# Layer 1 of a two-layer graph attention: two rows of 2048 values made on 128x16 tiles and carried by transfers

## What is computed

```
Wh  = h @ W                              # (B, 2048, 256)
s_i = Wh @ a[:256]                       # a node's own term
s_j = Wh @ a[256:]                       # its term as a neighbour
e   = leaky_relu(s_i[:, :, None] + s_j[:, None, :], 0.2)
e   = where((adj > 0) | eye, e, -inf)
h'  = elu(softmax(e, -1) @ Wh)
out = layernorm(h + h')
```

## Time and profile before

| | |
|---|---|
| median of 3 runs | 4035.5 us (4033.26 to 4039.04) |
| the profiled execution | 4037.52 us |
| its span, first to last instruction | 4035.0 us |
| mean granted TensorE clock | 0.975 |
| layer 0 | to about 2698 us |
| start of layer 1: mask and first batch's preparation | 2698 to 2813 us |
| layer 1's eight batches | 2813 to 4035 us |
| one batch | about 156 us |
| busy over the whole span | PE 3749.1, DVE 3096.8, ACT 2503.3, POOL 2038.1 us |

### The profile page before, as it was taken

How to read it: one execution, slowest core, us unless ns; L and a number is a source line. 1 busy time by engine, 2 the same in 40 slices (tenths; PEclk the granted TensorE clock), 3 DMA queues, 4 the chain that set the end, 5 groups by cost and what they waited for, 6 DMA issues and landing times. The chain is left out here.

```text
span 4035.0 us, 71120 instructions
## 1 busy us (share of the span) xinstructions
PE 3749.1 (93%) x25476; PEld 1764.5 (44%) x25476; DVE 3096.8 (77%) x4053; ACT 2503.3 (62%) x3554; POOL 2038.1 (51%) x1068
## 2 busy tenths in 40 slices
PE   6999999999999999999999999952998998899998
PEld 1333323333323332332333333321776777777777
DVE  6676777677577677677767757858889889899897
ACT  3565656566666566566656566631676776776777
POOL 1776777677677677677767768842011011011010
PEclk9999999999999999999999999976999999999999
DMA  5000000001000000000000100023110110111101
GB/s 213 1 32 12 22 33 12 12 14 41 12 12 32 22 12 33 12 22 33 12 12 13 42 12 12 22 96 139 32 53 26 49 53 22 53 40 35 32 24 39
DMA packets 106437, 141.08 MB, mean 35 GB/s; under 512 B 3793, under 2 KB 87633, under 8 KB 104017
## 3 DMA queue, kind: packets, MB, share of 16 engines
q1 hardware_dynamic: 104816, 135.80, 10.1%
q10 hardware_dynamic: 1248, 0.40, 0.1%
HBM read 102.63 MB, written 33.55 MB: 34 GB/s over the span
## 5 line engine op out<-in xcount | busy, mean ns | idle before, releaser
L368 ACT ACTIVATE probs<-probs 128x1024 f32<-128x1024 f32 x1024 | 1080.4, 1055 | 945.9 <-DVE probs L621 915.4
L621 DVE SCALAR_TENSOR_TENSOR probs<-sc_ps,clip_hi 128x1024 f32<-128x1024 f32 x1024 | 1203.2, 1216 | 572.8 <-PE sc_ps L446 568.9
L267 POOL TENSOR_TENSOR psums<-probs 128x1024 f32<-128x1024 f32 x512 | 1246.6, 2457 | 163.4 <-ACT probs L368 163.4
L1075 PE MATMUL out_ps<-wh,e 128*128 128x257 f32 x4096 | 964.6, 389 | 166.0 <-DVE e L1217 159.9
L446 PE MATMUL sc_ps<-q_cols,k_cols 64*128 64x512 f32 x4096 | 1022.3, 617 | 25.1 <-DVE probs L621 12.6
L462 PE MATMUL ctx_ps<-probs,v_rows 128*32 128x512 f32 x8192 | 977.3, 595 | 1.2 <-DVE seg_ctx L544 1.2
L1075 PEld LDWEIGHTS out_ps<-wh,e 128*128 128x128 f32 x4096 | 778.1, 193 | 326.8 <-DVE e L1217 120.6
L278 POOL TENSOR_TENSOR ctx_t<-ctx_t,seg_ctx 128x1024 f32<-128x1024 f32 x224 | 534.2, 2385 | 604.5 <-DVE seg_ctx L544 604.4
L446 PEld LDWEIGHTS sc_ps<-q_cols,k_cols 64*128 64x128 f32 x4096 | 353.1, 186 | 698.0 <-issue 575.4
L904 POOL TENSOR_TENSOR rstd<-var_eps,minus_half 128x4 f32<-128x4 f32 x32 | 68.4, 2138 | 1069.9 <-DVE var_eps L1177 1069.9
L462 PEld LDWEIGHTS ctx_ps<-probs,v_rows 128*32 128x32 f32 x8192 | 255.8, 110 | 597.8 <-issue 550.2
(11 more groups left out here) (85 smaller groups left out, 2393.8 us busy)
## 6 DMA issues: line engine op xcount, KB each, us to landing
x_cols<-in_xT SPq DMA_DIRECT2D x8, 2048.0 KB, 10.2
probs<-in_adjT SPq DMA_DIRECT2D x16, 1024.0 KB, 8.4
x_rows<-in_x SPq DMA_DIRECT2D x32, 512.0 KB, 4.8
x<-res SPq DMA_DIRECT2D x32, 512.0 KB, 3.3
x_in<-x SPq DMA_DIRECT2D x8, 2048.0 KB, 10.9
x_res<-x SPq DMA_DIRECT2D x32, 512.0 KB, 4.6
out<-h SPq DMA_DIRECT2D x32, 512.0 KB, 3.2
e<-in_adjT SPq DMA_DIRECT2D x8, 1024.0 KB, 7.9
```

The costliest lines, as they stand in the source:

```text
L267: pool.tensor_tensor(psums[:, q % 2, pair, :], probs[:, (SJ * q) % RING, pair, :], probs[:, (SJ * q + 1) % RING, pair, :], ALU.add).then_i ...
L368: act.activation(probs[:, n % RING, pair, :], probs[:, n % RING, pair, :], ACT.Exp, scale=DH ** -0.5).then_inc(s_exp, 1)
L621: dve.scalar_tensor_tensor(out=probs[:, n % RING, pair, :], in0=sc_ps[:, p, :, :], scalar=-LIM, in1=clip_hi[:, j, c * CW:(c + 1) * CW][:, ...
L1075: last = pe.matmul(out_ps[:, bank(c, t), 0:F + 1], e[:, n % ERING, t * P:(t + 1) * P], wh[:, p, j, 1:F + 2], start=(j == 0), stop=(j == JB ...
```

## The change

The own terms s_i are no longer made by products of their own. W a1 becomes one more column of w_ext, so that each of the 16 products for wh has 258 columns and gives s_i beside s_j, with i along the partitions (wh[:, p, j, 0]). The four uses of PE, ACT's four copies and s_row are gone. SyncE carries s_i to memory, as 2048 single values, and back as a 128x16 tile with node 16 q + r in partition q (`spread_own`, in chunk 2). After the reduction it carries the maxima out of partition 0 of low into the same form, m_c (`make_rows`, in the last chunk). VectorE does the four row operations on 128x16, all behind step 54. SyncE then stores the two rows in memory and loads each back into all 128 partitions, and ACT waits for these loads.

```diff
-    TU, WU, SU = KB * NC, JB, NC
-    USES = TU + WU + SU
+    TU, WU = KB * NC, JB
+    USES = TU + WU
+    RJ = N // P
...
-    ROWS_AT = (53, 55, 57, 59)
+    ROWS_AT = 54
...
+            def spread_own(b):
+
+                sp.wait_ge(s_prepread, count(b, USES, 2 + TU + WU))
+                with nc.allow_non_contiguous_dma(reason="2048 values a batch"):
+                    sp.dma_start(s_d[0].rearrange("(j p) -> p j", p=P), wh[:, b[1] % 2, :, 0]).then_inc(s_sout, 16)
+                sp.wait_ge(s_sout, count(b, 16, 16))
+                sp.dma_start(s_c[:, :], s_d[0].rearrange("(p j) -> p j", p=P)).then_inc(s_sin, 16)
+
+            def make_rows(b):
+                p = b[1] % 2
+                sp.wait_ge(s_all, count(b, 1, 1))
+                sp.dma_start(m_c[:, :], low[0:1, p, :].rearrange("o (q j) -> o q j", j=RJ)).then_inc(s_m, 16)
+                sp.wait_ge(s_rows, count(b, 4, 4))
+                sp.dma_start(rows_d.rearrange("r (p j) -> p r j", p=P), rows_c[:, :, :]).then_inc(s_rout, 16)
+                sp.wait_ge(s_rout, count(b, 16, 16))
+                sp.dma_start(best[:, p, :], rows_d[0].partition_broadcast(P)).then_inc(s_rin, 16)
+                sp.dma_start(low[:, p, :], rows_d[1].partition_broadcast(P)).then_inc(s_rin, 16)
...
+                    if c == 2 and more:
+                        spread_own(following(b))
+                    if c == NC - 1 and more:
+                        make_rows(following(b))
...
-                    act.wait_ge(s_rows, count(b, 4, 4))
+                    act.wait_ge(s_rin, count(b, 32, 32))
...
-                else:
-                    c = u - TU - WU
-                    for k in range(KB):
-                        last = pe.matmul(prep_ps[:, u % 2, :], wa1_b[:, k, :],
-                                         x_cols[:, k, c * CW:(c + 1) * CW],
-                                         start=(k == 0), stop=(k == KB - 1))
...
                 if k == 0:
-                    dve.wait_ge(s_prepread, count(b, USES, 2 + USES))
-                    dve.wait_ge(s_all, count(b, 1, 1))
-
-                    dve.tensor_tensor(low[:, p, :], low[:, p, :], s_row[:, :], ALU.add).then_inc(s_rows, 1)
+                    dve.wait_ge(s_sin, count(b, 16, 16))
+                    dve.wait_ge(s_m, count(b, 16, 16))
+                    dve.tensor_tensor(m_c[:, :], m_c[:, :], s_c[:, :], ALU.add).then_inc(s_rows, 1)
...
-                            if n in ROWS_AT:
-                                row_operation(following(b), ROWS_AT.index(n))
+                            if n == ROWS_AT:
+                                for k in range(4):
+                                    row_operation(following(b), k)
```

More of the change, by code:

```diff
@@ L681, in _, with layer1 @@
             run(dve, prologue, chunk, tail)
-def layer1(nc, x1, adjT, W, a, out):
+def layer1(nc, x1, adjT, W, a, s_d, rows_d, out):
     B, N, F = x1.shape
@@ L759, in layer1 @@
         x_cols = sb("x1_cols", [P, KB, N])
-        wh = sb("wh", [P, 2, JB, F + 2])
+        wh = sb("wh", [P, 2, JB, F + 3])
         s_fifth = sb("s_fifth", [P, 2, JB])
-        s_row = sb("s_row", [P, N])
+        s_c = sb("s_c", [P, RJ])
+        m_c = sb("m_c", [P, RJ])
+        rows_c = sb("rows_c", [P, 2, RJ])
         best = sb("best", [P, 2, N])
@@ L863, in prologue @@
                 load_x((0, 1))
+                spread_own((0, 0))
+                make_rows((0, 0))
             def steps(b, chunks, prev, more):
@@ L1024, in _ @@
             pe.wait_ge(s_id, 4)
-            pe.wait_ge(s_wa, 2 * KB + KB)
+            pe.wait_ge(s_wa, 2 * KB)
             def prepare(b, u):
@@ L1092, in _ @@
             for k in range(KB):
-                for i, (row, dst) in enumerate(((a1_r, wa1[:, k:k + 1]), (a2_r, w_ext[:, k, 0:1]))):
-                    dve.tensor_tensor_reduce(out=trash[:, 2 * k + i, :], in0=w_ext[:, k, 1:F + 1], in1=row[:, :],
+                for i, (row, dst) in enumerate(((a1_r, w_ext[:, k, 0:1]), (a2_r, w_ext[:, k, 1:2]))):
+                    dve.tensor_tensor_reduce(out=trash[:, 2 * k + i, :], in0=w_ext[:, k, 2:F + 2], in1=row[:, :],
                                              scale=1.0, scalar=0.0, op0=ALU.mult, op1=ALU.add,
                                              accum_out=dst).then_inc(s_wa, 1)
[L1097 to L1101, removed]
             def mask_piece(i):
@@ L1123, in maximum @@
                 if j == 0:
-                    dve.tensor_scalar(best[:, p, :], mask[:, 0, :], wh[:, p, 0, 0:1], None, ALU.min)\
+                    dve.tensor_scalar(best[:, p, :], mask[:, 0, :], wh[:, p, 0, 1:2], None, ALU.min)\
                        .then_inc(s_best, 1)
@@ L1143, in row_operation @@
                     dve.wait_ge(s_rows, count(b, 4, 2))
-                    dve.tensor_tensor(best[:, p, :], s_row[:, :], low[:, p, :], ALU.subtract).then_inc(s_rows, 1)
+                    dve.tensor_tensor(rows_c[:, 0, :], s_c[:, :], m_c[:, :], ALU.subtract).then_inc(s_rows, 1)
                 if k == 3:
-                    dve.scalar_tensor_tensor(out=low[:, p, :], in0=s_row[:, :], scalar=ALPHA, in1=low[:, p, :],
+                    dve.scalar_tensor_tensor(out=rows_c[:, 1, :], in0=s_c[:, :], scalar=ALPHA, in1=m_c[:, :],
                                              op0=ALU.mult, op1=ALU.subtract).then_inc(s_rows, 1)
@@ L1256, in build @@
     layer0(nc, x, xT, adjT, wqT, wkT, wvT, woT, bq, bk, bv, bo, gamma, beta, x1)
-    layer1(nc, x1, adjT, W, a, out)
+    s_d = nc.dram_tensor("s_own", (1, x.shape[1]), F32, kind="Internal").ap()
+    rows_d = nc.dram_tensor("rows", (2, x.shape[1]), F32, kind="Internal").ap()
+    layer1(nc, x1, adjT, W, a, s_d, rows_d, out)
 def kernel(x, adj, L0_gnn_Wq, L0_gnn_bq, L0_gnn_Wk, L0_gnn_bk, L0_gnn_Wv, L0_gnn_bv, L0_gnn_Wo, L0_gnn_bo,
```

39 lines of the change are left out of this document (18 added, 21 removed).

## The result

| | before | after |
|---|---|---|
| median | 4035.9 us (4033.3 to 4039.0, 4 runs) | 3989.3 us (3986.9 to 3994.0, 4 runs) |
| profiled execution, span | 4037.5, 4035.0 us | 3986.9, 3985.0 us |
| mean granted TensorE clock | 0.975 | 0.972 |

The ratio is 0.9886, with a 95% interval of 0.9868 to 0.9903: 46.7 us by the medians, 50.0 us between the two profiled executions. 3996 us was forecast, with 3979 to 4024 as the range.

A forecast was written before the change was run, and what follows sets the result against it. Row operations, ACT, VectorE's masks and TensorE in turn were taken to bound each batch boundary. Boundaries -48.3, clock +5, start +4.0 and nothing exposed at L = 10.5 gave -39.3 us: 3996 us, range 3979 to 4024.

The forecast's parts named there:

- The chain at the boundary: Last chunk: row operations, then ACT, VectorE's masks, TensorE set the time; shortening the row operations gains 6.9 us a boundary.
- The two bounds that I found close together: At a boundary: ACT after nmr lets PE go on at 3279.9; TensorE's own unbroken work needs until 3280.24.
- L: Time from the last row operation to the rows' landing in all partitions: 10.5 us, of which store 2.2, load 8.3.
- the factor of 1.35 for the shared source: In the load: all partitions reading one place lengthens the bytes' time, from packets of 64 ns against 48.
- The hidden part: At each boundary L may be 10.9 us at no cost; each us above costs a us at seven boundaries.
- The rival of the slow shared reads: Rival (3): the two loads from one place run under 190 GB/s; at 134, L 19.7, +31.5, 4067 us; chance 0.11.
- the prediction's formula: Whole change: -48.3 + 5 + 7 x max(0, L - 10.9) + (L - 6.5); zero at L = 15.8.
- The products at no gain: Third chunk: TensorE's 16 removed instructions a batch gain nothing, as PE catches up during VectorE's 4.09 us mask at step 49.
- The clock: TensorE's new idle pieces before steps 44 and 49 bring low-clock stretches at three boundaries more: +5 us (0 to +12).
- The start: Start of layer 1, before the first batch: nothing hides the chain of transfers, L - 6.5 = +4.0 us.
- SyncE's queue: Two added waits, all hidden: own terms' store takes 3 to 16 us, with 21.9 us free before chunk 1's store.

The follow-up runs named there:

- the run with short row operations: The kernel before, its four row operations on 16 of 2048 columns, no transfer added: 3977.9 us, ratio to before 0.9856.
- the small store twice: The changed kernel with the store of the two rows done a second time after the first has landed: 3996.3 us, ratio 0.9907.
- Loads made twice: The changed kernel with the two loads into all partitions done again after the first pair has landed: 4038.2 us, ratio 1.0006.
- the products kept: The changed kernel with TensorE's four uses for the own terms and ACT's four copies put back, result unused: 3989.2 us, ratio to before 0.9882.

## Why the prediction was right

**The chain at the boundary** (row operations, ACT, masks, TensorE) was the right reading. 6.9 us a boundary were forecast. The last chunks gave 7.1 and the first chunks behind them another 0.13. The two bounds that I found close together, nmr at 19.77 us behind the reciprocals and TensorE unbroken, are both in the trace: 19.37 us, and PE at work from 3238.65 to 3269.17. That the chain without transfers gives this gain, the run with short row operations shows.

**L** was forecast at 10.5 us and measured 8.6 to 9.5 (16.7 to 17.6 us less 8.07; this counts to ACT's start, some 0.2 us behind the landing). The store took 1.6 and not 2.2 us, the load 7.0 to 8.0 and not 8.3. The mistake in this term was the factor of 1.35 for the shared source. It came from rows of 1 KB, and at 8 KB there is none. The 64 and 48 ns were means over 104 and 173 packets, with those of 4 bytes among them: of both kinds most packets of 1 KB lasted 46 ns, and a few long ones made the difference. The hidden part was forecast at 10.9 and is 10.2. The landing was hidden by 0.7 to 1.6 us, so at the boundaries these errors did not reach the sum. In part that is luck: at the L of 10.5 that I took, 0.3 us a boundary would have shown. And the chain was one store of 1.6 us from showing, as the small store twice has it.

**The rival of the slow shared reads** (3) did not come about at 8 KB. Its mechanism is real, though, and shows at 2 KB. At the 108 GB/s that the 2 KB loads had, 2 MB would take 19.4 us (an estimate), and by the prediction's formula the change would have lost. Loads made twice took the gain to nothing at a mean L of 16.7; the formula had put this point at 15.8.

**The products at no gain** held, from both sides, and so did the reason: VectorE's stall at step 49. I gave 2.7 us a boundary as the price if that cover were gone; it is 0.8 (5.3 over seven).

**The clock** was the term that was mis-sized: +5 us were set aside. There are more low stretches now, 17 in the batches against 11, but three last chunks that are 1.1 to 1.4 us longer are followed by first chunks that are 0.8 us shorter. That is under 2 us in all: 1.3. With the products kept all seven last chunks take 26.6 to 26.7 us, and its boundaries are 1.2 us shorter in sum. The other new stretches lie in second and third chunks, and the third ones did not get longer.

**The start**: +4.0 forecast, +3.0 measured. The chain that the sum describes cost 2.3 us (L was 8.8 there, not 10.5). The other 0.7, GpSimd's longer wait before the reduction, is no term of it; in the kernels with these transfers and one store of the own terms that wait is 5.6 to 6.6 us, and before it was 5.6.

By terms, the forecast was -48.3 + 5 + 4.0 = -39.3; measured in the profiles -50.5 with the clock's share in it, +3.0, and -2.4 in places that the sum has no term for (second chunks, and what stands ahead of the reduction at the start). The median of all runs moved by 46.7.

**SyncE's queue**: the store of the own terms took 10.8 us on average (10.4 to 11.2), between the 3 and 16 forecast, and the stores of chunks were not held up.

## What to carry to other kernels

Before work is moved from an engine to transfers, follow the chain from its last input to its first reader and count what of it lies beside other work; here 10.2 us did, and 8.6 to 9.5 were used. Look at which of two equally busy engines waits in the stretch concerned: 7.5 us of TensorE's work per batch were worth nothing as long as another engine's stall closed the stretch. And when one small row is to go to all partitions, load it in runs of 6 or 8 KB, as measured here, and not in runs of 2.

## What the hardware showed that I had not expected

- All 128 partitions reading the same 8 KB: packets of 314 ns, 424 GB/s, as fast as from different places (309 ns). Reading the same 2 KB: packets of 268 ns, 108 GB/s; reading 2 KB each from different places: 99 ns. The Trainium skill (DMA: Bandwidth & Descriptors, "Latency and other measured facts") has copies slow down when the rows of the partitions lie a large power of two apart, down to 103 GB/s. The transfers looked at here have no such distances; at a distance of zero, rows of 8 KB moved at 424 GB/s and rows of 2 KB at 108.
- The reduction over the partitions on GpSimd makes one VectorE operation last 4.1 us instead of 0.68, in each batch that prepares a next one; without it such a batch is 2.7 us shorter.
- 2048 single values of 4 bytes are stored in 10.8 us on average, 5.3 ns each.
- GpSimd stands 5.5 to 6.0 us between a small instruction and the reduction behind it at every boundary of the changed kernel. With stores in runs of 4 bytes under way in that time it stood 7.5 to 10.5 us.
